# Graph attention on one core: the outer product of VectorE moved between the first two running maxima, the mask copies moved to ScalarE

## The reference

```python
def _L1_gnn_ref(feat, efeat, W_msg, b_msg, W_attn, b_attn, src, dst):
    w_m = (efeat @ W_msg + b_msg).reshape(E, in_f, -1)
    w_a = (efeat @ W_attn + b_attn).reshape(E, in_f, -1)
    h_src = feat[src][:, :, None]
    e1 = w_m * h_src
    e2 = w_a * h_src
    seg_max = jax.ops.segment_max(e2, dst, num_segments=N)
    ex = jnp.exp(e2 - seg_max[dst])
    denom = jax.ops.segment_sum(ex, dst, num_segments=N)
    attn = ex / denom[dst]
    ft = jax.ops.segment_sum(e1 * attn, dst, num_segments=N)
    return ft.sum(axis=1)
```

## Time and profile before

| | |
|---|---|
| three runs | 10052.5, 10056.12, 9998.29 us (median 10052.5) |
| the profiled execution | 10031.8 us |
| its span, first to last instruction | 10029.9 us |
| mean granted TensorE clock | 0.860 of full speed |
| DVE busy | 7418.3 us (74%) |
| PE busy | 7095.5 us (71%) |
| POOL busy | 4523.9 us (45%) |
| ACT busy | 1793.4 us (18%) |

### The profile page before, as it was taken

The page is one execution under the profiler, slowest core; times in us unless marked ns, Lnnn a source line. Parts: engine busy times, 40 slices in busy tenths (PEclk is TensorE's granted clock), DMA queues, the critical chain, the costliest instruction groups (busy, mean ns, idle before and its releaser), DMA issues.

```text
span 10029.9 us, 229505 instructions
## 1 busy us (share of the span) xinstructions
PE 7095.5 (71%) x89519; PEld 6562.7 (65%) x89519; DVE 7418.3 (74%) x14398; ACT 1793.4 (18%) x3861; POOL 4523.9 (45%) x4625
## 2 busy tenths in 40 slices
PE   5888865666666666666666618888668888588884
PEld 5777755666666666666666517777667777477774
DVE  6666658999999999999999946666556566355654
ACT  0000003433334343333333310000000000000000
POOL 3555554333333333333333355555545555455554
PEclk9899887777777788777787759999889999799997
DMA  2222213333333333333333321111111111111110
GB/s 80 66 66 69 63 38 89 119 116 116 118 115 119 115 117 117 115 120 115 118 117 115 118 68 37 38 41 38 28 36 38 37 41 38 27 38 37 38 40 21
DMA packets 809009, 747.18 MB, mean 74 GB/s; under 512 B 217376, under 2 KB 769120, under 8 KB 808896
## 3 DMA queue, kind: packets, MB, share of 16 engines
q1 hardware_dynamic: 649088, 653.49, 20.0%
q0 software_dynamic: 154864, 90.47, 6.0%
q10 hardware_dynamic: 5008, 2.59, 0.1%
HBM read 229.59 MB, written 519.73 MB: 75 GB/s over the span
## 4 chain that ended last, share of the span: by engine, by line
PE 46%; DVE 31%; issue 18%; POOL 3%; DVEq 1%; DMA 1%; ACT 0%; ACTq 0%; SPq 0%; POOLq 0%; another core or an unknown queue 0%
PE ps L732 42%; DVE ps L846 7%; DVE amax_room L1115 6%; DVE spare L1120 4%; DVE z_room L846 3%; DVE flat L1148 3%; DVE flat L846 3%; PE ps L782 2%; POOL got L437 2%; DVE stt L846 2%; PE ps L775 1%; DVE spare L1128 1%; POOL wide_buf L437 1%; DVEq L1114 0%; POOL flat L437 0%
## 5 line engine op out<-in xcount | busy, mean ns | idle before, releaser
L437 POOL DMA_INDIRECT msg<-feat,cidx x2016 | 1975.8, 980 | 1854.5 <-PE ps L732 690.0
L437 POOL DMA_INDIRECT hsrc<-feat,aidx x1568 | 1518.9, 969 | 2674.6 <-DMA aidx<-src_sorted 2280.5
L732 PE MATMUL ps<-parts,wide_buf 128*128 128x112 bf16 x37632 | 2131.2, 217 | 713.5 <-issue 434.9
L732 PEld LDWEIGHTS ps<-parts,wide_buf 128*128 128x128 bf16 x37632 | 1970.5, 100 | 862.6 <-issue 858.4
L732 PE MATMUL ps<-parts,flat 128*128 128x112 bf16 x37632 | 2123.1, 217 | 423.3 <-issue 411.5
L732 PEld LDWEIGHTS ps<-parts,flat 128*128 128x128 bf16 x37632 | 1967.9, 100 | 568.1 <-issue 560.6
L775 PE MATMUL ps<-idm,z_room 128*102 128x128 f32 x4704 | 1101.8, 359 | 1430.7 <-DVE flat L846 1203.6
L782 PE MATMUL ps<-wsb,zT 102*128 102x192 f32 (+1 forms) x9408 | 2092.6, 377 | 16.1 <-ACT zT L645 11.9
L782 PEld LDWEIGHTS ps<-wsb,zT 102*128 102x128 f32 x9408 | 2002.1, 247 | 33.0 <-ACT zT L645 21.6
L775 PEld LDWEIGHTS ps<-idm,z_room 128*102 128x102 f32 x4704 | 688.5, 168 | 1646.6 <-issue 729.2
L846 DVE TENSOR_TENSOR raw<-ps,amask 128x1792 f32<-128x1792 f32 x224 | 453.6, 2025 | 1770.0 <-PE ps L732 1186.4
(11 more groups left out here) (210 smaller groups left out, 4253.4 us busy)
## 6 DMA issues: line engine op xcount, KB each, us to landing
state_tab<-flat SPq DMA_DIRECT2D x784, 512.0 KB, 3.3
raw<-quot_tab SPq DMA_DIRECT2D x224, 512.0 KB
run_tab<-run SPq DMA_DIRECT2D x224, 224.0 KB
top_tab<-spare SPq DMA_DIRECT2D x392, 128.0 KB
msg<-feat,cidx POOLq DMA_INDIRECT x2016
hsrc<-feat,aidx POOLq DMA_INDIRECT x1568
efs<-in_ef SPq DMA_DIRECT2D x392, 34.0 KB
msg<-in_x,cidx POOLq DMA_INDIRECT x672
```

The source lines that it names most:

```text
L437: return pool.indirect_dma_start(dest, None, table, rows_at(idx))
L732: last = nc.tensor.matmul(slot[s][:, t, 0:QW].rearrange("p (q c) -> p q c", c=D), hot[s][:, m, t * P:(t + 1) * P], parts[:, m * Q:(m + 1) ...
```

## The change

It does four things, all in the attention:

1. The outer product leaves the head of `step` and stands between the first and the second running maximum.
2. The mask copy leaves VectorE. ScalarE makes it (`masks`), behind the fourth `turned` of the same group and ahead of the second piece of `weights`; a new semaphore `a_ring` tells VectorE, which waits for it ahead of its first maximum.
3. The maxima no longer wait for one product each. The first waits for products 0 and 1 (`products(j, s, HG)`, `HG` = 2), the third for all four. The weighting by the second piece moves from behind the third maximum to behind the second, the rescaling stays between the third and the fourth.
4. The waits whose values need a register (`a_mm`, `a_w`, `a_put`) are written ahead of the waits on VectorE's own results (`need`). The waits on `a_sum` that protected the mask buffer now stand ahead of the rescaling.

```diff
@@ act @@
+            def masks(j, s):
+                nc.scalar.activation(aring[:, s], resets[:, :, bass.ds((2 * j + s) * G, G)], ACT.Copy).then_inc(a_ring[s], 1)
+
             def group(j, s):
                 b, jb = 1 - s, j - 1 + s
                 for k in range(G):
                     if k == G - 1:
                         weights(jb, b, 0)
                     turned(j, s, k)
+                masks(j, s)
                 weights(jb, b, 1)
@@ dve @@
-                def ring_copy(j, s):
-                    return v.tensor_copy(aring[:, s], resets[:, :, bass.ds((2 * j + s) * G, G)])
-
-                def running_max(j, s, k):
-                    dve.wait_ge(a_mm[s], j * G + k + 1)
+                def products(j, s, n):
+
+                    dve.wait_ge(a_mm[s], j * G + n)
+
+                def running_max(s, k):
                     return mark(v.scalar_tensor_tensor(amax[:, s, k, :], amax[:, 1 - s, G - 1, :] if k == 0 else amax[:, s, k - 1, :],
                                                        aring[:, s, 0, k:k + 1], logits[s][:, k, :], ALU.add, ALU.max))
...
                 def step(j, s, ahead, again, put_before):
 
                     b, jb = 1 - s, j - 1 + s
+                    weighted(jb, b, 0)
+                    dve.wait_ge(a_ring[s], j + 1)
+                    products(j, s, HG)
+                    m = running_max(s, 0)
                     if ahead:
                         outer(jb + 1, b)
-                    weighted(jb, b, 0)
+                    need(m)
+                    m = running_max(s, 1)
+                    weighted(jb, b, 1)
+                    products(j, s, G)
+                    need(m)
+                    m = running_max(s, 2)
                     if again:
                         dve.wait_ge(a_sum[s], j * G)
-                    need(mark(ring_copy(j, s)))
-                    m = running_max(j, s, 0)
-                    need(m)
-                    m = running_max(j, s, 1)
-                    need(m)
-                    m = running_max(j, s, 2)
-                    weighted(jb, b, 1)
                     r = rescaled(jb, b)
                     need(m)
-                    m = running_max(j, s, 3)
-                    need(r)
+                    m = running_max(s, 3)
                     if put_before:
                         dve.wait_ge(a_put[b], 32 * jb)
+                    dve.wait_ge(a_w[b], 2 * jb + 2)
+                    need(r)
                     running_sum(jb, b, 0)
```

More of the change, by code:

```diff
@@ L292, in gnn_program @@
         a_sum = ring("a_sum")
+        a_ring = ring("a_ring")
         a_put = ring("a_put")
@@ L665, in _ @@
                 turned(0, 0, k)
+            masks(0, 0)
             group(0, 1)
@@ L1143, in running_sum @@
                     if k == 0:
-                        dve.wait_ge(a_w[s], 2 * j + 2)
                         out = tt(st[:, s, 0, :], stt[:].rearrange("p t c -> p (t c)"), bank, ALU.add)
@@ L1192, in attention @@
                 loop_start()
[L1193 to L1198, removed]
+                dve.wait_ge(a_ring[0], 1)
+                dve.wait_ge(a_mm[0], G)
+                for k in range(G):
+                    need(running_max(0, k))
                 differences(0, 3, 4)
                 for k in range(G - 2, -1, -1):
-                    m = segment_max(0, k)
-                    need(m)
+                    need(segment_max(0, k))
                 differences(0, 2, 3).then_inc(a_d[0], 1)
@@ L1219, in attention @@
                 dve.wait_ge(a_put[1], 32 * (AHALF - 1))
+                dve.wait_ge(a_w[1], 2 * AHALF)
                 for k in range(G):
```

## The result

| | before | changed |
|---|---|---|
| median of the runs, us | 10054.31 (4 runs) | 10413.06 (4 runs) |
| lowest to highest, us | 9998.29 to 10067.31 | 10392.84 to 10454.94 |
| profiled execution: span, us | 10029.9 | 10453.1 |
| granted clock over the span | 0.860 | 0.820 |
| attention, first to last "first running sum", us | 4184.5 | 4570.7 |

The ratio is 1.0361, with a 95% interval of 1.033 to 1.0391: 359 us by the medians, forecast 10,380 against 10,413 measured.

What follows compares the result with a forecast made beforehand. VectorE's full queue was taken to bound the attention; the change makes a three-engine loop of 11.59 us a step, 0.88 x 390 = 343 us on 10031.8, giving 10,375, rounded 10,380; range 10,110 to 10,620.

Steps and rivals of the forecast that it cites:

- The saving on VectorE: VectorE's attention step without waits: 0.72 us less, 9.99 left; 0.29 for the copy, twice 0.215 for dependent maxima.
- closed loop: Attention step, sum to fourth tile to masks to maximum to sum: 11.37 us with old class shares, 0.66 more.
- The two classes: Attention steps by start of ScalarE's fourth tile: middle (T + 0.97) 11.09 us, late (T + 1.97) 12.09.
- T: Start of an attention step; the first running sum of the step before lies at T - 5.42 us.
- The mix of clocks: TensorE in the attention: idle 3.7 us, early groups (tile by T + 0.45) go, step 11.59 us, 343 us more.
- Rival (b): Attention: TensorE starts each group at half clock, 12.09 us a step, 10,570 us in all; chance 0.16.
- Where the waits stand: VectorE's attention step: 1.2 to 1.7 us idle ahead of first maximum, up to 1.2 ahead of first weighting.
- a sign of being wrong: Attention: prediction fails if the mask copy is not what ends VectorE's wait, or if the clock rises; no size.
- The register waits: VectorE's queue: a register instruction carrying the wait costs 0.09 us each time it ends last; inside the 0.72 saving.
- The mask copy by the Trainium skill's budget: ScalarE's mask copy in the attention: 0.31 us by budget against the row's 0.212, 39 us higher; the row decided.
- Rival (a): VectorE's saving arrives whole, 9.99 us a step, 9,751 us; needs a fourth tile by T - 0.13; chance 0.08.
- Costed at nothing: Attention: outer product up to 2.7 us later, cover 2.3; mask copy delays second exponentials by 0.2; no cost.

Runs made afterwards that it cites:

- experiment 6: Changed kernel with one transpose and one product matmul an edge instead of three, PSUM cleared once; 273 us less than the kernel before, ratio 0.9713.
- experiment 5: The changed kernel measured again, unaltered; 392 us more than the kernel before, ratio 1.0388.
- experiment 1: Changed kernel with the maxima's half of the masks copied at the head of ScalarE's group; 27 us less than the kernel before, ratio 0.9969.
- Experiment 4: Kernel before with only the register waits (`a_mm`, `a_w`, `a_put`) written ahead of `need`; 22 us less than the kernel before, ratio 0.9975.

## Why the prediction was right

**The saving on VectorE** (0.72 a step, 9.99 left) was right: experiment 6 shows 9.97. **That it runs into a closed loop** of sum, transposes, fourth tile, masks, maximum was right, piece by piece: fourth tile to first maximum 0.73 forecast, 3526.91 - 3526.20 = 0.71 measured where the masks alone hold it (the 0.73 of the step of 3514.10 is the weighting's as much as theirs); maximum to sum 3.97, 3518.80 - 3514.83 = 3.97; ScalarE's mask copy 0.21 forecast, 0.200 measured. The two classes came out where they were put: the step of 3514.10 is a middle one, 11.13 against 11.09, and the late ones, whose fourth tile starts at T + 1.9 or later, take 12.1 against 12.09. But they hold only 55 and some 165 of the steps: in another 166 the tile starts between T + 1.1 and T + 1.9, 1.40 in the mean, and these take 11.51.

**The mix of clocks** was the step with judgement in it, and its direction was right: TensorE idle 3.80 us ahead of a group in the step shown (3.7 forecast), early groups gone (none of 387 left), clock down from 0.79 to 0.73. The size was slightly off: halfway between middle and late gave 11.59, the profiled execution shows 11.69, experiment 5 11.59. Rival (b), all groups late, did not come: in the step of 3514.10 the clock was back at full by the last transposes (0.49).

```profile
3507.00:3508.00 1.00, 0.00 (x0) 1.00 0.26 35
...
3509.00:3510.00 1.00, 0.54 (x4) 0.60 0.10 8
3510.00:3511.00 1.00, 1.00 (x5) 0.50 0.00 0
3511.00:3512.00 1.00, 1.00 (x5) 0.50 0.08 8
3512.00:3513.00 1.00, 1.00 (x7) 0.70 0.11 8
3513.00:3514.00 1.00, 1.00 (x10) 1.00 0.46 129
```

These are windows of 1 us of the changed kernel, with the granted clock behind the busy time: full while TensorE was idle, half from some 3509.2, full again from some 3512.6. The Trainium skill's rule ("TensorE: Matmul & The Clock Gate", "What's actually happening"), that activity releases the throttle, and the trace agree in kind: it took the group's own work to bring the clock back. But the clock had stayed full while TensorE was idle, and fell when work had begun again.

The reason given for the mix, the length of the idle time, is not borne out. In the changed kernel TensorE is idle 3.23 to 3.84 us ahead of every group, and of 386 groups 165 began at full clock (their first three transposes take 0.51) and 221 at half (0.88, as at 3519.53). The start does not decide the class either: those that began at full clock took 11.77 us a step in the mean, as 110 of the 165 fell to half before their last transposes, and those that began at half took 11.65. So rival (b) had its condition in over half of the groups and not its price, and that halfway between middle and late came so near was in part luck.

**Where the waits stand** was forecast wrongly. I put 1.2 to 1.7 us ahead of the first maximum and up to 1.2 ahead of the first weighting; measured are 0.48 a step and 1.04. The sum, 1.52, is near the 11.59 - 9.99 = 1.60 of the forecast, since in a loop the first wait that binds takes what the later one would have shown. But the prediction named it a sign of being wrong if the mask copy was not what ends VectorE's wait, and it ends only a third of it; the exponentials, which the forecast took for the smaller part, end the rest. That also misled me in experiment 1, where I took the 0.48 for what the masks cost.

**The register waits.** "A register instruction that carries the wait costs 0.09 each time that it ends last" was read from two places that also differ in what the instruction itself waits for. Experiment 4 gives 0.03 at the copy and 0.02 at each dependent maximum. It did not matter for the forecast, as the changed order hides it, but the number was wrong.

**The mask copy by the Trainium skill's budget** ("ScalarE: Activation LUTs", "Rules for kernel authors"), an estimate of 0.31, is too high here: 0.200 measured. The budget is stated for an ACTIVATE whose bias is a pointer operand, and `masks` gives none, so it was the wrong price to hold beside the row.

**The early steps of before.** Rival (a) rested on a fourth tile at T - 0.13 or earlier, "which no step of before shows". Four of 384 do, at T - 0.29 (one at 4530.24, with its outer product at 4530.53). It changes no figure of the forecast.

**Costed at nothing.** Nobody waited for the outer product, as forecast: in none of the 387 steps of the loop does VectorE wait for a gathered row ahead of its outer product.

## What to carry to other kernels

An operation that needs nothing new and stands ahead of one that waits is cover, even if no wait shows beside it; before moving it, look up when the results behind it really arrive, against their new place, step by step and for both levels of the clock, and not by a mean. Where an engine's full queue hides a chain through other engines that comes back to it, shortening the queue beyond the chain wins nothing, and each operation put into the chain lengthens every step. Waits inside such a loop don't add up: only taking one away shows its price (here about 1.0 us where the trace showed 0.48).

## What the runs showed of the hardware

The kernel before took 10,054 us on one chip and 8,706 on another, which I had not expected. The attention is alike (its step 10.70 on the first; experiment 4, 0.02 to 0.03 faster in three places, 10.64 on the other). The difference is TensorE's time at one line of the other layers, whose code is the same: line 732 with its two source tiles in the kernel before, first chip, and then in experiment 4, second chip:

```profile
L732 PE MATMUL ps<-parts,wide_buf 128*128 128x112 bf16 x37632 | 2131.2, 217 | 713.5 <-issue 434.9
...
L732 PE MATMUL ps<-parts,flat 128*128 128x112 bf16 x37632 | 2123.1, 217 | 423.3 <-issue 411.5
```

```profile
L732 PE MATMUL ps<-parts,wide_buf 128*128 128x112 bf16 x37632 | 1876.6, 213 | 293.4 <-DVE wide_buf L1000 293.4
...
L732 PE MATMUL ps<-parts,flat 128*128 128x112 bf16 x37632 | 1868.8, 213 | 28.7 <-DVE flat L1000 28.7
```

Idle time that waited for nothing the profile shows, 434.9 and 411.5 us, is gone on the second, and the line is busy for 509 us less. Busy and idle time together fall by 1324 us, which is all that the stretches outside the attention differ by (5845 us on the first chip, 4521 on the second). These are runs of 336 matmuls written out one by one; what holds them back on the first chip was not tried.

In experiment 6 VectorE's instructions lasted longer than elsewhere (a sum of 128x512 0.855 us at the median against 0.680), while their starts stood as close as ever (9.97 a step). A duration is not what an instruction takes of its queue. Why they lasted longer there was not tried either.
